# Layer 3's gated convolution: from DVE taps over channels to three shifted products over tokens

## The reference, cut to what matters

```python
def bit_linear(x, w):                      # forward value
    return act_quant(x) @ weight_quant(w).T
# act_quant: per token, round(x * s) / s with s = 127 / max|x|, clipped to -128..127
# weight_quant: per matrix, entries -1, 0, 1 times mean|w|
h = bit_linear(x, w1)                      # 128 -> 512 channels
y = depthwise_conv1d(h over the 256 tokens of a batch, conv_w (512 x 3), padding 1) + conv_b
y = silu(y)
out = bit_linear(y, w2)                    # 512 -> 128, act_quant over the 512 channels of a token
```

## Time and profile before

| | |
|---|---|
| median of three runs | 1088.63 us (1088.04 to 1097.9) |
| the profiled execution, its own time | 1088.47 us |
| its span | 1086.3 us, so 2.2 us lie around it |
| granted PE clock, mean | 0.919 of full speed |
| busy: PE, DVE, ACT, POOL | 950.2, 728.9, 557.3, 502.8 us |
| first product of the stage, last residual of the stage | 1012.10 us, ends at 1083.55 us |

### The profile page before, as it was taken

How to read it: one execution, slowest core, us unless ns; L and a number is a source line. 1 busy time by engine, 2 the same in 40 slices (tenths; PEclk the granted TensorE clock), 3 DMA queues, 4 the chain that set the end, 5 groups by cost and what they waited for, 6 DMA issues and landing times.

```text
span 1086.3 us, 15531 instructions
## 1 busy us (share of the span) xinstructions
PE 950.2 (87%) x4485; PEld 716.7 (66%) x4485; DVE 728.9 (67%) x1602; ACT 557.3 (51%) x1077; POOL 502.8 (46%) x512
## 2 busy tenths in 40 slices
PE   5699799999999686999999999999996779966564
PEld 3577566656669482688888888888864746635353
DVE  7677455546554478666666666666756888867796
ACT  2355466666550324666666666666641334433684
POOL 6012222223321310377777777777753449973200
PEclk9899899999999898999999999999997679988566
DMA  5000000003210000000000000000001000000001
GB/s 174 1 1 2 1 1 1 1 1 97 72 53 2 25 1 0 21 25 28 22 24 27 22 22 28 22 22 28 19 0 59 1 0 1 1 1 1 1 10 29
DMA packets 26964, 22.90 MB, mean 21 GB/s; under 512 B 3403, under 2 KB 23971, under 8 KB 26787
## 3 DMA queue, kind: packets, MB, share of 16 engines
q1 hardware_dynamic: 26915, 22.30, 6.9%
HBM read 21.24 MB, written 1.05 MB: 21 GB/s over the span
## 4 chain that ended last, share of the span: by engine, by line
PE 73%; DVE 17%; POOL 3%; ACT 3%; issue 2%; DMA 0%; SPq 0%; DVEq 0%; ACTq 0%
PE psum L1710 66%; DVE stats L1189 1%; PE psum L1832 1%; PE psum L1840 1%; PE psum L1780 1%; POOL rstd L586 1%; DVE xn L1202 1%; DVE arena L1265 1%; POOL hh L666 1%; PE psum L1729 1%; DVE mv L1192 1%; PE psum L1903 1%; DVE arena L1660 1%; DVE arena L1661 1%; DVE arena L1667 1%
## 5 line engine op out<-in xcount | busy, mean ns | idle before, releaser
L1710 PE MATMUL psum<-xall,wgu 128*128 128x512 f32 x1424 | 390.8, 408 | 16.8 <-POOL wgu L624 9.8
L1710 PEld LDWEIGHTS psum<-xall,wgu 128*128 128x128 f32 x1424 | 272.7, 194 | 88.2 <-issue 25.6
L632 POOL TENSOR_TENSOR hh<-arena,hh 128x512 fp32r<-128x512 f32 x176 | 227.9, 1295 | 81.4 <-ACT hh L762 80.1
L1710 PE MATMUL psum<-hh,wdn 128*128 128x512 f32 x672 | 197.0, 399 | 5.4 <-ACT hh L762 3.5
L1499 DVE TENSOR_TENSOR psum<-psum,arena 128x512 f32<-128x512 f32 x176 | 123.0, 699 | 98.4 <-PE psum L1710 92.1
L985 ACT ACTIVATE arena<-psum 128x512 f32<-128x512 f32 x176 | 105.3, 598 | 131.5 <-PE psum L1710 131.4
L762 ACT ACTIVATE hh<-arena 128x512 fp32r<-128x512 f32 x224 | 140.3, 626 | 46.5 <-DVE arena L1627 43.4
L1710 PEld LDWEIGHTS psum<-hh,wdn 128*128 128x128 f32 x672 | 126.5, 189 | 45.9 <-POOL hh L666 16.1
L1504 DVE TENSOR_TENSOR arena<-psum,arena 128x512 f32<-128x512 f32 x176 | 121.6, 691 | 7.6 <-DVE psum L1499 1.7
L1710 PE MATMUL psum<-arena 128*128 128x18 f32 (+7 forms) x776 | 122.0, 317 | 5.3 <-DVE X L1581 2.6
L762 ACT ACTIVATE arena<-psum 128x1024 f32<-128x1024 f32 (+9 forms) x118 | 79.7, 687 | 90.4 <-PE psum L1710 30.1
(11 more groups left out here) (281 smaller groups left out, 1383.1 us busy)
## 6 DMA issues: line engine op xcount, KB each, us to landing
egu<-in_w SPq DMA_DIRECT2D x44, 128.0 KB, 2.0
egu<-in_egu SPq DMA_DIRECT2D x16, 256.0 KB, 2.7
edn<-in_w SPq DMA_DIRECT2D x44, 64.0 KB, 1.8
edn<-in_edn SPq DMA_DIRECT2D x16, 128.0 KB, 2.1
arena<-in_w SPq DMA_DIRECT2D x1, 1536.0 KB, 7.1
X<-in_x SPq DMA_DIRECT2D x4, 256.0 KB, 4.0
out<-X SPq DMA_DIRECT2D x4, 256.0 KB, 2.3
arena<-in_ctxTd SPq DMA_DIRECT2D x1, 512.0 KB, 5.2
```

Of the source, the lines that this page charges most:

```text
L632: pool.tensor_tensor(hh[:, s % 4, 1, :], h1[:, s % 2, :], hh[:, s % 4, 0, :].bitcast(F32), ALU.subtract).then_inc(hh_lo, 1)
L1710: return pe.matmul(dst, lhsT=lhsT, rhs=rhs, start=start, stop=stop)
```

## The change

- **Weights.** The three kernels w1q * mean|w| * conv_w[k] (128 x 512 each) are made once by DVE (`w3f`), behind the last `hidden2` of layer 2; ACT rounds them to fp32r behind the copies of `o2T` (`hh[:, k, 0]`, and the bias row `cbias`), POOL subtracts for the low parts behind the bias of X in layer 6 (`hh[:, k, 1]`). `convB`, conv_w and conv_b on every partition, comes with one more DMA behind `w2all`; ACT waits for both.
- **Tokens.** `xpad` (in the place of `xall` and the start of `wgu`) holds the turned tokens with a zero column before and behind each batch, so a tile shifted by one token is a slice.
- **Products.** `first3(t)`: one tile of 128 tokens stationary, 512 channels moving, ten products in one bank: the bias, per tap the high tokens with the high and the low weights, per tap the low tokens with the high weights. Four banks (0, 1, 4, 5).
- **Behind it.** Silu from PSUM into `gt` (`activated`), the scale from `gt`, the scaled pair from `gt`, integers, and as before. `unit_in`, `convolve`, `unit_out`, `hidden_T` are gone; a pair's steps are one turn and two turns behind its products, outputs three.
- **First product.** `token_low(0)` stands behind tile 15's residual ahead of the last statistics; `token_integers(0)` ahead of the statistics of group 2; POOL scales group 0 within group 1; PE turns group 1 after the first two tiles' products.

```diff
                 if L == 6:
...
+                    for k in range(3):
+                        pool.wait_ge(w3_hi, k + 1)
+                        pool.tensor_tensor(hh[:, k, 1, :], w3f[:, k, :], hh[:, k, 0, :].bitcast(F32), ALU.subtract).then_inc(w3_lo, 1)
...
             sp.dma_start(w2all, A["w2"]).then_inc(w2_in, 16)
+            sp.dma_start(convB, A["conv"].partition_broadcast(P)).then_inc(w2_in, 16)
...
-            act.wait_ge(w2_in, 16)
+            act.wait_ge(w2_in, 32)
...
+            act.wait_ge(w3_made, 1)
+            for k in range(3):
+                copy(hh[:, k, 0, :], w3f[:, k, :]).then_inc(w3_hi, 1)
+            copy(cbias, convB[0:C, 3, :]).then_inc(w3_hi, 1)
...
-            for turn in range(TURNS3):
+            for turn in range(PAIRS + 2):
+                if turn < PAIRS:
+                    activated(2 * turn)
                 if turn in (1, 2):
                     token_scale(turn + 1)
+                if 1 <= turn <= PAIRS:
+                    scaled_pair(turn - 1)
+                if turn >= 2:
+                    integers_in(turn - 2)
+                if turn < PAIRS:
+                    activated(2 * turn + 1)
+                if turn < NG - 1:
                     token_high(turn + 1)
...
             def norm_behind(L, t):
+                if L == 7 and t == NT - 1:
+                    token_low(0)
                 if t % 4 == 3:
+                    if L == 7 and t // 4 == 2:
+                        token_integers(0)
                     ln_stats(L, t // 4)
-                    if L == 7 and t >= 8:
-                        token_integers(t // 4 - 2)
+                    if L == 7 and t // 4 == 3:
+                        token_integers(1)
...
+            dve.wait_ge(w2_in, 32)
+            dve.wait_ge(wq_done, 2)
+            for k in range(3):
+                last = dve.tensor_tensor(w3f[:, k, :], wa[:, 0, :], convB[:, k, :], ALU.mult)
+            last.then_inc(w3_made, 1)
             output_groups(6, NG)
...
+            def outputs3(q):
+                dve.wait_ge(l2_ready, q + 1)
...
+            for turn in range(PAIRS + 3):
                 if turn == 1:
                     token_integers(3)
-                if turn in (1, 2):
-                    token_low(turn + 1)
-                if 0 <= turn - 4 < PAIRS:
-                    integers(turn - 4)
-                if 0 <= turn - 3 < PAIRS:
-                    quant_scale(turn - 3)
-                if 2 * turn < UNITS:
-                    convolve(2 * turn)
-                    convolve(2 * turn + 1)
+                if turn in (2, 3):
+                    token_low(turn)
+                if turn >= 3:
+                    outputs3(turn - 3)
+                if 1 <= turn <= PAIRS:
+                    quant_scale(turn - 1)
+                    integers(turn - 1)
...
+            def first3(t):
+                g, at = t // 4, (N + 2) * (t // 2) + P * (t % 2)
+                pe.wait_ge(xq_lo, g + 1)
+                if t >= 4:
+                    pe.wait_ge(g3_done, t - 3)
+                into = bank(L1_BANKS[t % 4])
+                mm(into, share, cbias, True, False)
+                for k in range(3):
+                    for half in range(2):
+                        mm(into, xpad[:, 0, at + k:at + k + P], hh[:, k, half, :], False, False)
+                for k in range(3):
+                    last = mm(into, xpad[:, 1, at + k:at + k + P], hh[:, k, 0, :], False, k == 2)
+                last.then_inc(l1_ready, 1)
...
+            for turn in range(PAIRS + 2):
+                if turn == 1:
+                    pe.wait_ge(x_done, 7 * NT)
+                if turn < PAIRS:
+                    first3(2 * turn)
+                if turn >= 2:
+                    integers_T(turn - 2)
+                if turn < PAIRS:
+                    first3(2 * turn + 1)
+                if turn < NG - 1:
                     tokens_T(turn + 1)
+                if turn >= 2:
+                    output3(turn - 2)
```

More of the change, by code:

```diff
@@ L1110, in _ @@
             load_table(ACT.Silu)
-            act.wait_ge(wq_done, 1)
-            copy(w1r, w1q)
             def token_scale(g):
@@ L1122, in token_high, with activated, scaled_pair, integers_in @@
                 act.wait_ge(xq_tp, g + 1)
[L1123 to L1140 removed]
+                copy(padded(0, g), bank(2 + g % 2).rearrange("p (b n) -> p b n", b=2)).then_inc(xq_hi, 1)
+            def activated(t):
+                q, k = t // 2, t % 2
+                act.wait_ge(l1_ready, t + 1)
+                if q >= 2:
+                    act.wait_ge(ga_done, q - 1)
+                act.activation(gt[:, q % 2, k, :], bank(L1_BANKS[t % 4]), ACT.Silu).then_inc(g3_done, 1)
+            def scaled_pair(q):
+                act.wait_ge(qs4_done, q + 1)
+                if q >= 2:
+                    act.wait_ge(gi_done, q - 1)
+                for k in range(2):
+                    last = act.activation(ga[:, q % 2, k, :], gt[:, q % 2, k, :], ACT.Copy, scale=qs4[:, 2 * q + k:2 * q + k + 1])
+                last.then_inc(ga_done, 1)
+            def integers_in(q):
+                act.wait_ge(gi_tp, q + 1)
+                if q >= 2:
+                    act.wait_ge(l2_ready, q - 1)
+                copy(giT[:, q % 2].rearrange("p c n -> p (c n)"), bank(6).bitcast(BF16)).then_inc(gi_sb, 1)
             token_scale(0)
```

170 lines of the change are left out of this document (49 added, 121 removed).

## The result

The changed kernel takes 1078.03 us, median of four runs (1074.27, 1074.77, 1081.3, 1083.05), beside 1089.24 us for the kernel before on the same chip. In two later sets of runs the same kernel took 1075.44 and 1073.90 us (ratios 0.9866, interval 0.9823 to 0.9909, and 0.9853, interval 0.9810 to 0.9895). The profiled execution took 1074.77 us with a span of 1073.0; the prediction was 1073.4, with 1069 to 1081 as its range, and the median lies 4.6 above it.

What follows compares the result with a forecast made beforehand. DVE was taken to set the pace in the last stage, at 6.6 us a turn. From 1088.47 us, 16.1 saved there and 1.0 added for preparation gave 1073.4, range 1069 to 1081.

Steps and rivals of the forecast that it cites:

- a turn over 6.3: Last stage: named sign that the prediction would be wrong, reduction to reduction over 6.3 us instead of 5.8.
- Preparation: Ahead of layer 2's outputs: DVE's three weighted kernels add 1.0 us, held until POOL is through; possible range 0 to 2.1.
- First scale at 1017.3: Stage opening: DVE's scale of pair 0 starts at 1017.3, after POOL's scaling of group 3 and its integers.
- First output products end at 1027.9: Stage opening: a chain of scales, scaled pairs, integers and ACT's copy brings the first output products to 1027.9.
- PE is not what the first output waits for: Stage opening: DVE's and POOL's work delays the first output; PE's first product may be some 3 us late for free.
- Second output, 7.0 behind the first: After the opening: one turn of 5.8 plus 1.2 for group 3's low part, its high part behind an activation.
- The turn, 5.8 predicted: Last stage: one pair of token tiles takes 5.8 us against 6.6; PE's own need 5.5 to 5.8 at full clock.
- the predicted ring: Each turn: output products, DVE's output and scale, ACT's scaled pair and integer copy set the pace, 5.73 us.
- The tail, 6.55 from the scaled pair 7 to the last X: Stage end: today's 7.1 us less a 0.55 wait of PE gives 6.55, last X at 1067.5.
- Clock: Last stage: PE reaches 2.4 GHz some 5 us after its start and keeps it through short gaps.
- The two clock rivals: Last stage: clock comes and goes as today, 1086, chance 0.07; PE never gets its clock, 1105.7, chance 0.04.
- The turn stays at 6.6: Last stage rival: costlier hand-overs or shifted weight slices leave only opening and end gains, 1078 to 1079; chance 0.07.

Runs made afterwards that it cites:

- e1: Changed kernel without each tile's bias product, so nine wide products instead of ten; 1075.43 us, turn 5.59.
- e2: Changed kernel with the bias product contracting 128 rows, 64 of them zero, instead of 64; 1073.82 us, turn 5.83.
- g2: Changed kernel with 128-row bias product, reordered last turn and 16 extra products nothing reads, placed where PE waits anyway; 1070.69 us.
- g3: Changed kernel with the three weighted kernels made by POOL, ACT rounding before the exponentials, DVE's low bias part behind the softmax; 1075.02 us.
- f3: Changed kernel with the three weighted kernels made one by one in the middle of layer 2's experts; 1077.62 us.

## Why the prediction was right, and where it was off

The time lies in the range, and the change of bottleneck, the clock and the kind of gain came as forecast. One sign that the prediction named for being wrong did come: a turn over 6.3. The profiled execution took 1.4 us more than 1073.4. Step by step:

- **Preparation, 1.0 predicted, 0.47 measured.** DVE's three products took 3.79 instead of 2.1, and POOL's last two 2.96 instead of 2.51, so they did hold each other. DVE's first output starts at 960.16, 0.70 behind PE's turning as before the change (0.71), and PE's last expert product waits for POOL; but DVE's three products end at the same moment (956.42 + 3.79). Either would give about the 0.47, and no run parts them. The exclusive lock that the Trainium skill describes ("SBUF — State Buffer", "Who interferes with whom") agrees with the trace in kind: both sides took longer. The prediction let only DVE pay for it. ACT's roundings and POOL's subtractions were hidden, as forecast: ACT still waits 2.96 us ahead of the layer norm's copy at 966.91.
- **First scale at 1017.3.** It was 26.1 us behind the first residual of the attention; 26.2 was predicted. Right in time. DVE had waited 0.92 us for ACT's high part of group 1 just before, behind a Silu that waited for PE; with shorter tiles (e1, e2) the scale came at 25.8.
- **First output products end at 1027.9.** 37.2 behind the first residual against 36.8. The number is right by chance: the chain that was named would have ended them at 36.0, as in e2, and PE's work added 1.2.
- **"PE is not what the first output waits for", and a late start "worth nothing" up to some 3 us.** Wrong. The step counted two tiles on PE against DVE's scale, but six tiles and the turned groups stand in PE's order ahead of the first output products, and ACT's scaled pair and copy stand behind the Silu of the fifth.
- **Second output, 7.0 behind the first.** It was 6.36: the late high part cost nothing beside PE.
- **The turn, 5.8 predicted, 6.36 measured.** This is the term that was mis-sized. PE's 20 wide products were all priced at the experts' 0.22, 4.4 in all; measured they take 5.26 (2 x 0.44 and 2 x 2.19). The small groups, 1.1, were right. e2 shows that 0.66 of the miss is the 64-row bias product alone; without the change of rows PE needs 5.7, inside the predicted 5.5 to 5.8. That e2's turn is then 5.83 is not the predicted ring: it is set by the loop through one tile on PE and ACT's Silu, which the prediction did not name, and the predicted ring of 5.73 set the pace in no run (in e1 the turn was 5.59).
- **The six turns from the first output to the seventh: 37.2 us against 36.0** (7.0 + 5 x 5.8). Five turns at 0.56 over the price are 2.8 too many; the 1.2 charged for the late high part and the last turn, 5.46 without wide products, gave 1.5 back. That these misses offset each other is luck, and without it the sum would be further off.
- **The tail, 6.55 from the scaled pair 7 to the last X.** Measured 1063.33 to 1070.31, 7.0: PE's clock was low there, and the output products of pair 6 took 1.03.
- **Clock.** Predicted to rise some 5 us behind the start and to stay. It rose 5.6 behind it and stayed at 1.00 to the end of the wide products. The two clock rivals did not happen; g2 shows what one fall costs, 1.6 us in nine products, with 2 estimated.
- **Sum.** From the first residual of the attention to the end of the last one, 76.4 us were predicted (991.06 to 1067.5) and 78.5 measured (991.83 to 1070.31). Of the 2.0, 0.3 is the opening, 1.2 the turns, 0.4 the output products of pair 6 at the low clock. Ahead of it the changed kernel lay 0.8 behind before and not 1.0, and 0.4 of that was there at the experts' first weighted product already (879.91 against 879.49); around the span 1.8 us instead of 2.2. So 1.4 in all.

"The turn stays at 6.6" is closer to the measured turn than the forecast's 5.8: 6.36, though by neither of the two causes that it named. Why nine products of 128 rows take 0.233 each here and 0.225 in the experts was not tried. Nor was why the medians of one kernel differ by 4 us between the three sets; the fall of the clock ahead of layer 3, seen in g3's trace, is a candidate.

## What to carry to other kernels

When work is moved to an engine, count in its own order all that it must pass before the product somebody waits for, not only the work of that step. Then do the same for the engine that waits for it: where ACT's copy stood behind a Silu that waits for PE, the wait was named after ACT and was PE's. Price a product by its rows as well as its columns: a bias product over 64 rows between products of 128 was dearer than one padded to 128. Before a gap is used to hide work, ask whether the engine's next instruction there is on a chain: idle time of DVE inside the experts' loop was not free (f3), POOL's ahead of the softmax was (g3).

## What the runs showed of the hardware that was not expected

- A product over 64 rows among products over 128 stopped the loading of weights ahead: the next load came 0.43 us behind the 64-row one and not 0.11, and a tile's ten products and one small group took 3.18 us instead of 2.85.
- DVE's products of two SBUF tiles and POOL's subtractions slowed each other both ways: 3.79 for 2.1 and 2.96 for 2.51.
- Slices shifted by one token as the stationary operand cost nothing (turn 6.37 without the shift, 6.35 with it).
- The rise of PE's clock came 5.6 us behind a start at 1007.45 and some 3.5 behind one at 1012.96, and 0.85 us of the delay was given back in this way. In layer 3's projections the same ten products took 5.69 to 5.78 us in ten traces and 5.43 in an eleventh.
- The clock can fall in one launch of a kernel and not in the next: sixteen products ahead of every edit took 12.90 us at 0.50 in the trace of g3 and 7.13 in all others.
